# Quantised attention stage: one-pass products of whole numbers with split weights, and chunk biases multiplied once per chunk

## The reference, cut to the stage that is changed

The program is a decoder of six sublayers over 64 sequences of 64 rows with 256 columns, each followed by a residual and a layer norm. The change touches the fourth, attention with 32 heads of width 8 whose four projections (q, k, v, o) are quantised. The rows are cut into chunks of 32; a chunk has one bias per column (the middle of its range), and a scale per column that is the chunk's top divided by a power of two.

## Time and profile before

| | us |
|---|---|
| median of 3 runs | 2873.56 (2867.43 to 2874.4) |
| span of the profiled execution | 2871.8 |
| changed block: first to last `turn_x` | 1946.3 to 2387.1 |
| its loop, 13 turns | 1993.1 to 2387.2 |
| PE busy, whole program | 2677.8 (93%) |
| DVE busy | 1878.6 (65%) |
| ACT, POOL busy | 1313.3 (46%), 1247.7 (43%) |

### The profile page before, as it was taken

One profiled execution on the slowest core, in us unless ns is written; L12 is line 12 of the kernel. 1 busy time (PEld: TensorE's weight loads), 2 busy tenths in 40 slices (PEclk: granted clock), 3 DMA queues, 4 the chain that ended last, 5 costly groups with the idle time before them and its releaser, 6 DMA issues. The chain is left out here.

```text
span 2871.8 us, 65100 instructions
## 1 busy us (share of the span) xinstructions
PE 2677.8 (93%) x23764; PEld 2313.3 (81%) x23764; DVE 1878.6 (65%) x4020; ACT 1313.3 (46%) x3143; POOL 1247.7 (43%) x1619
## 2 busy tenths in 40 slices
PE   7999999996999999999999799997999998699995
PEld 7999999985888888888888688885777777477774
DVE  5665556655777777777777554445777777366666
ACT  3222222224666666666666533322333343266655
POOL 2211212223767676777767401113554554334434
PEclk9999999998999999999999899998999998799998
DMA  5000000001000000000000110001000000000001
GB/s 185 8 7 7 7 4 7 7 8 53 4 5 4 5 4 5 4 4 5 4 5 4 44 32 0 0 0 33 9 12 7 8 11 0 26 31 28 25 10 59
DMA packets 43308, 49.17 MB, mean 17 GB/s; under 512 B 4064, under 2 KB 33632, under 8 KB 42976
## 3 DMA queue, kind: packets, MB, share of 16 engines
q1 hardware_dynamic: 43232, 48.16, 5.0%
HBM read 35.56 MB, written 4.19 MB: 14 GB/s over the span
## 5 line engine op out<-in xcount | busy, mean ns | idle before, releaser
L587 POOL TENSOR_TENSOR a_probs<-a_probs,a_rs 128x512 f32<-128x512 f32 x64 | 70.7, 1105 | 466.3 <-DVE a_rs L443 466.3
L1173 POOL TENSOR_TENSOR b_rows<-b_rows,b_swapped 128x512 f32<-128x512 f32 x160 | 204.7, 1288 | 57.2 <-DVE b_swapped L946 57.2
L1108 ACT ACTIVATE b_probs<-bank,b_shift,b_q_scale 128x128 f32<-128x128 f32 x512 | 228.4, 461 | 0.6
L1220 POOL TENSOR_TENSOR b_probs<-b_probs,b_rs 128x512 f32<-128x512 f32 x128 | 133.4, 1042 | 136.7 <-DVE b_rs L998 133.5
L2657 ACT ACTIVATE d_probs<-d_probs 128x512 f32<-128x512 f32 x128 | 78.9, 630 | 240.5 <-DVE d_probs L2556 238.6
L531 ACT COPY a_pT<-bank 128x512 f32<-128x512 f32 x64 | 37.5, 586 | 308.4 <-PE bank L324 308.4
L448 DVE TENSOR_TENSOR a_oT<-bank,a_oT 128x512 fp32r<-128x512 f32 x128 | 82.5, 687 | 143.6 <-ACT a_oT L536 143.6
L1183 POOL TENSOR_TENSOR b_rms<-b_rms,sh_minus_half 128x8 f32<-128x8 f32 (+1 forms) x128 | 170.6, 1333 | 10.7
L954 DVE TENSOR_REDUCE b_ss<-b_squares 128x4 f32<-128x512 f32 x192 | 125.3, 680 | 73.9 <-ACT b_squares L1083 73.9
L46 PE MATMUL bank<-a_xT,early_wq 128*128 128x256 f32 x512 | 150.2, 293 | 13.1 <-DVE early_wq L73 10.3
L46 PE MATMUL bank<-early_wo,b_oT 128*128 128x256 f32 x512 | 150.4, 294 | 1.4 <-DVE b_oT L920 1.4
(11 more groups left out here) (350 smaller groups left out, 8940.2 us busy)
## 6 DMA issues: line engine op xcount, KB each, us to landing
a_xT_in<-in_xT SPq DMA_DIRECT2D x16, 256.0 KB, 2.6
sh_x<-in_x SPq DMA_DIRECT2D x1, 4096.0 KB, 18.8
b_ctx_in<-in_ctxT SPq DMA_DIRECT2D x32, 128.0 KB, 2.0
d_x_in<-sh_x SPq DMA_DIRECT2D x16, 256.0 KB, 2.3
e_x_in<-sh_x SPq DMA_DIRECT2D x16, 256.0 KB, 2.4
e_cT<-in_ctxT SPq DMA_DIRECT2D x32, 128.0 KB, 2.5
out<-sh_x SPq DMA_DIRECT2D x16, 256.0 KB, 2.1
a_qT<-in_L_attn_Wq SPq DMA_DIRECT2D x4, 512.0 KB, 5.9
```

The costliest lines, as they stand in the source:

```text
L1108: op = act.activation(probs[:, g % 2, keys], bS[:, keys], ACT.Exp, bias=shift[:, g % 2, a:a + 1], scale=q_scale[:, g, a // 2, a % 2:a % 2 ...
L1173: pool.tensor_tensor(rows[:, unit, :], rows[:, unit, :], swapped[:, half, :], ALU.add).then_inc(added[unit], 1)
L1220: pool.tensor_tensor(pr, pr, rs[:, g % 2, :].unsqueeze(2).to_broadcast([128, R, 128]), ALU.mult).then_inc(probs_ready[g], 1)
```

```diff
+                k = q.reps // M
+                dve.tensor_tensor(q.cmax[:, :, :, :], q.copies(q.up[:, :], k), q.copies(q.down[:, :], k), ALU.max).then_inc(q.cmax_ready, 1)
...
                 for c in range(C):
-                    op = pe.transpose(bank[0:M, c * 128:(c + 1) * 128], q.cmax[:, c * M:(c + 1) * M], sh.ident[:, :])
+                    op = pe.matmul(bank[0:q.reps, c * 128:(c + 1) * 128], q.cmax[:, c, :, :].rearrange("p k m -> p (k m)"),
+                                   sh.ident[:, :], start=True, stop=True)
+                for c in range(C):
+                    bias = q.bias[:, c, :, :].rearrange("p k m -> p (k m)")
+                    for j, m in enumerate(weights):
+                        op = pe.matmul(bank[32 * j:32 * j + 32, YB], bias, w[:, m, c, :], start=(c == 0), stop=(c == C - 1))
                 op.then_inc(q.cmax_turned, 1)
...
+                pe.wait_ge(q.top_ready, this(i))
+                pe.wait_ge(y_read, this(i))
+                for k in range(3):
+                    op = pe.matmul(bank[:, k * M:(k + 1) * M], q.top[0:M, k:k + 1].to_broadcast([M, 128]), sh.ident[0:M, 0:M], start=True, stop=True)
+                op.then_inc(q.top_spread, 1)
...
+            def exact(out, left, right, start):
+                pe.matmul(out, left[0], right[0], start=start, stop=False)
+                return pe.matmul(out, left[1], right[1], start=False, stop=False)
+
+            def project_columns(bank, m, o):
+                out = bank[:, o * 256:(o + 1) * 256]
+                for c in range(C):
+                    exact(out, parts(lambda a: wq[:, m, a, c, o * 128:(o + 1) * 128]), (qx.result[:, c, :], qx.result[:, c, :]), c == 0)
+                return pe.matmul(out, qx.y_both[:, o * 128:(o + 1) * 128], of_chunk[:, m, :], start=False, stop=True)
...
-                    pe.matmul(bank[:, r * D:(r + 1) * D], result[:, c, r * 128:(r + 1) * 128], wq[:, m, c, :], start=(c == 0), stop=False)
-                for c in range(C):
-                    op = pe.matmul(bank[:, r * D:(r + 1) * D], bias[:, c, r * 128:(r + 1) * 128], w[:, m, c, :],
-                                   start=False, stop=(c == C - 1))
+                    exact(out, (q.result[:, c, rows], q.result[:, c, rows]), parts(lambda a: wq[:, m, a, c, :]), c == 0)
+                return pe.matmul(out, of_chunk[0:q.reps, lane, rows], q.y_both[:, :], start=False, stop=True)
...
+                dve.tensor_tensor(y_sum[:, :], bX[1][0:96, YB], y_rows[:, :], ALU.add).then_inc(y_summed, 1)
...
+                dve.scalar_tensor_tensor(q.y_both[:, :], q.y_high[:, :].bitcast(F32), keep_low[0:q.reps, :], q.y_whole[:, :],
+                                         ALU.mult, ALU.add).then_inc(q.y_both_ready, 1)
...
             def turn(new, mid, old, oldest):          # DVE
...
                 find_top(new, qx, bX[1])
                 centre(new, qx, bX[0])
+                unit(new, qx)
                 widest(old, qc)
+                invert_unit(new, qx)
+                sum_y(new)
+                smallest(new, qx)
                 shift(mid, 5)
-                thresholds(new, qx, bX[1])
+                thresholds(new, qx)
                 maximum(mid, 7)
+                find_top(old, qc, bX[0])
                 maximum(mid, 6)
-                add_bias(new)
-                find_top(old, qc, bX[0])
+                unit(old, qc)
+                both_y(new, qx, v_ready)
+                invert_unit(old, qc)
                 count(new, qx)
+                smallest(old, qc)
+                clip(new, qx)
                 shift(mid, 6)
+                invert(new, qx)
                 take_att(mid, 0, 2)
-                invert(new, qx)
-                thresholds(old, qc, bX[0])
                 divide(new, qx)
                 restore(new, qx, v_ready)
+                thresholds(old, qc)
+                shift(mid, 7)
+                both_y(old, qc, y_ready)
                 count(old, qc)
+                clip(old, qc)
+                take_k(new)
                 invert(old, qc)
                 divide(old, qc)
                 restore(old, qc, y_ready)
-                take_k(new)
-                shift(mid, 7)
-                take_q(new)
                 residual(old)
...
             def turn(new, mid, old, oldest):          # ACT
...
+                scale_y(new, qx, y_sum[:, :])
                 exponent(mid, 4)
+                high_y(new, qx)
+                take_top(new, qx, bX[1])
+                take_pT(mid, 4)
                 exponent(mid, 5)
-                take_pT(mid, 4)
+                scale_y(old, qc, bX[0][0:32, YB])
+                high_y(old, qc)
+                take_top(old, qc, bX[0])
                 take_pT(mid, 5)
+                exponent(mid, 6)
+                take_q(new)
```

326 lines of the change are left out of this document (209 added, 117 removed).

## The result

The kernel after takes **2999.6 us** (median of four runs, 2991.1 to 3001.9) against 2870.7 for the kernel before beside it: a ratio of 1.0447 with a 95% interval of 1.0428 to 1.0466. It is slower, as forecast, but by 129 us where the forecast had 25, and outside the range. The profiled execution spans 2998.6. The changed block carries it: from its first `turn_x` to the first load of the last block it took 527.7 before (1946.3 to 2474.0) and now 654.2 (1950.4 to 2604.6).

The account below looks back on a forecast made before the run. The prediction took a ring of short steps between engines as the bound: 12.95 + 3.25 + 7.08 + 7.1 = 30.4 us, plus 1.6 for the clock, 32.0 per turn. 14 turns with the ends add 25: 2899 us, range 2850 to 2940.

Parts of the forecast that it names:

- piece four: From the end of x's restoring to the next turn_x: 9.89 us falls to 7.1, spread_k hidden.
- a ring of hops: Changed block: a turn is bound by short steps hopping between PE, DVE, POOL and ACT, 29.84 us at full clock.
- faster: Rival, 17%: PE is the true bound and DVE's new waits fall into existing time; 28.6 us per turn, 2851 us total.
- clock as now: Rival, 20%: new gaps are short and PE keeps its clock grant; 0.56 us more per turn, 2883 us total.
- Piece two: From the start of find_top to the start of thresholds: 1.93 us grows to 3.25, DVE idle 0.9.
- six bias products in three groups: x's bias products on PE: groups of 32 rows overlap nearly fully, twelve instructions in 0.87 us, 2.6 otherwise.
- the last rival: Much slower, 18%: bias groups don't overlap (2923 us), or lower clock holds all through the turn's second half (2944 us).
- The form change left out: 32-row products among 128-row ones on PE: no drain charged for tiling mode changes; 0.4 us in sum otherwise.
- Piece three: From thresholds to the end of restore: 5.24 us grows to 7.1, DVE waiting 1.4 at find_top(old).
- Piece one: From turn_x to the start of find_top: 12.78 us becomes 12.95, PE reaching cmax 0.9 earlier, at 11.45.
- The clock, 1.6: Slow stretches of PE's lower clock lie on the chain: 1.6 us more per turn, bounds 0.45 to 4.8.
- The ends: First turn_x +1.6 us, first turn +1, last two turns -0.6 each; together +1.4.

Follow-up runs that it names:

- e1: Kernel after with take_k(new) moved back behind restore(old) on DVE: 2929.4 us, ratio 1.0223.
- e5: e1 with the output's bias rows made in 96 rows and three groups, so no 32-row product stands among those of 128: 2927.1 us, ratio 1.0203.
- e14: e1 with two of the eight transposes of the probabilities made twice and Q's products made three times: 2937.1 us, ratio 1.0236.
- e11: e1 with v copied without its scale: 2917.3 us, ratio 1.0163.
- e4: Kernel before with take_k(new) moved from behind the restoring to ahead of the division: 2888.1 us, ratio 1.0079.
- e2: Kernel after with five unused float32 products between Q and the output products, PE's wait for k_taken ahead of them: 2979.0 us, ratio 1.0399.
- e13: Kernel before with Q's float32 products made twice: 2877.7 us, ratio 1.0036.
- e8: Kernel before with restored values and quantised weights as fp32r, products in one pass, low parts left out: 2846.9 us, ratio 0.9937.

## Why the prediction was wrong, step by step

The step that failed is piece four: the overlap of `spread_k` on POOL with DVE's division and restoring, which I put at nothing. It measured 12.79 where I had 7.1. Without it, as e1 shows, the time is 2929, inside my range. The direction was not luck: with that overlap and all loss to the clock gone, the turn of 32.6 is still 2.3 longer than before.

- **That a ring of hops bounds the block, not PE:** right. PE's idle time grew from 2.6 to 8.5 in the turns read and the turn got longer; the rival "faster" is out. So is "clock as now": the loop was granted 0.806, from 0.944.
- **Piece two, 3.25:** 3.22 in every turn, DVE's wait 0.95 where I had 0.9.
- **The six bias products in three groups:** right; twelve instructions lie within 1.06 with their tail, and the next row starts 1.00 behind them, where I had 0.87. Of the last rival the part on the groups, that they don't overlap, is out. The other part, the lower clock through the second half of the turn, came half true: the turn read has it from 2180.4 to 2183.8, from 2187.3 to 2190.7 and from 2194.1 on, and the full clock between.
- **fp32r products 0.12 apart:** right at the full clock, 0.21 at the lower.
- **The form change left out, by the row:** wrong. At the lower clock the 32-row product starts 0.34 behind the one before it and the next one 0.51 behind it, where 0.21 is the rule: 0.43 each, two a turn, and at the full clock some 0.28 (e1, from 2169.65 to 2170.17). The row that I went by had held a price: by L2322, whose six instructions hold 0.73, two of that form are worth some 0.2 of L2279's 0.32 (an estimate), and I read the rest as none. The Trainium skill's sentence in TensorEngine Tiling, section Tiling Modes, that a change of the mode drains TensorE, fits these rows. By e5 it didn't decide the time.
- **Piece three, 7.1:** 7.32, though by luck, for two errors that cancel. At the full clock it is 6.72, and `find_top(old)` waits 1.14 there (e14), not 1.4; in the turn read it waits 2.25, because the output's bias products run at the lower clock, and the mean comes back to 7.32.
- **Piece one, 12.95:** failed. I let PE come to `cmax` 0.9 sooner because V was shorter. At the full clock it came 12.62 into the turn (e14, from 2076.68 to 2089.30), 1.2 later than I had it and later than before: the copies of v are scaled by row now and take 3.04, not 2.21, and PE waits 0.78 for them and 0.73 for the next copy. I had priced the scaled copy like the plain one. From there to `find_top` it is 1.74, where I had 1.5. Together that is 1.4, and the other 1.1 is the clock. Of the 1.4, e11 gives back 0.66 by the plain copy; what holds the rest no run shows.
- **Piece four, 7.1:** the step that failed, with 12.79 in the mean and 13.1 in the turn read. I had division and restoring of the old batch at 0.7 and 0.8 and `spread_k` "hidden by 0 to 0.1 us", as if POOL and DVE could not disturb each other. They took 2.33 and 2.26, and the output products started 8.53 behind the end of x's restoring (2187.58 to 2196.11), not 4.85. Then these took 3.4 to the residual's start, where I had 1.2 and 0.2 of tail: at the full clock, in e1 (from 2169.2), the same stretch is 2.0, so 1.4 of it is the clock and 0.6 was missing from my sum. The residual's two halves up to `turn_x` took 1.12, where I had 0.8. 3.7, 2.0 and 0.3 make 6.0 in this turn, 5.7 in the mean. Of the 3.7, 3.1 are the two operations, which e1 and e4 show; the rest is mostly that k was taken later than I had it: DVE waits 0.46 for PE's k products, which ran at the lower clock. My 4.85 was also 0.3 above its own terms (2.9, then 0.16, 0.7 and 0.8 make 4.56).
- **The clock, 1.6, bounds to 4.8:** the mechanism was right and the size wrong, since it wasn't independent of the rest. With k late a turn costs 34.02 against 32.63 at the full clock, so 1.4, near my 1.6. In the kernel after it is more: e2's fill alone gives 1.65 back. The clock falls at 2194.1, within the wait of 4.3, and stays low to 2204.3, past the output products, V, `turn_x` and the first scores.
- **The ends:** +1.4 forecast. The block grew by 126.5, 13 turns account for 110.8; the turns outside the loop hold the remaining 16 (the second takes 32.1, from 25.3, and from the last `turn_x` to the next block it is 95.4, from 87.1). The first `turn_x` comes 4.1 later, with a wait of 3.65 for `of_chunk`, where I had 1.6, but e13 has it 3.2 later without that table. The -0.6 that I gave each of the last two turns is -0.3 by its own terms.

What remains open: e14's full-clock turn is 32.6 against my 30.4. Piece one is 1.4 longer than I had it and piece four 1.3, and piece three 0.4 shorter. In piece four k's taking comes before the output products there (about 0.6), and the rest, some 0.6, may lie in the form changes and the second half of the residual; no run took it apart.

## What to carry to other kernels

Before a step is moved, list what its successor on another engine will then run beside: here a DVE operation, moved up past three others, started POOL on top of two operations with both inputs in SBUF. That cost 4.8 us a turn, with what it did to the clock. When an edit makes PE's work shorter, read how long PE will stand idle ahead of the chain's own products; a gap of 2.5 us ahead of them ate most of e8's gain, and repeating products in it nearly tripled the gain. Test the parts of such a change apart: one of its parts alone, with a fill and without the low parts of the numbers, was 1.8% faster, the whole 4.5% slower.

## What the runs showed that I had not expected

- DVE and POOL hold each other up one instruction at a time: 0.69 becomes 2.26 to 2.41, and which of the two is hit depends on 0.1 to 0.2 us of start. POOL's pair grows from 3.75 to between 4.19 and 4.67.
- An ACT copy of 64x128 with a scale per row takes 0.38 (3.04 for eight), a plain one 0.28 (2.21 for eight).
- In e14 the same list of instructions gives turns of 32.6 to 36.5 that come back every six turns, by where the lower clock falls. A fill that is right for one turn is wrong for the next.
- Twelve repeated fp32r products made e8's turn 2.0 us shorter; the same idea in the kernel before, four float32 products, made it 0.9 longer in the mean and 0.6 at the full clock.
